# Decoder layer on one core: a deeper pipeline for the attention groups, the maxima turned eight heads at once and split by GpSimd

## The chip, the cores and the metric

One core of one Trainium2 chip runs the whole program. The metric is device time in microseconds (us) of one launch. TensorE (PE) does matrix products and transposes, VectorE (DVE) and ScalarE (ACT) read PSUM and SBUF, GpSimd (POOL) works from SBUF, and the queue of SyncE (SP) issues nearly all DMAs in program order.

## The reference, cut to what matters

Sixteen sequences of 256 tokens, width 256, go through one layer: self-attention with a per-head bias on the key's position, cross-attention over 120 context rows with a mask, and a mixture of eight experts of which each token takes two. A layer norm follows each part.

```
scores = einsum('bqhd,bkhd->bhqk', q, k) / 4 + alibi[h, k]      # 16 heads of depth 16
x = layernorm(x + softmax(scores) v Wo + bo)
x = layernorm(x + cross_attention(x, ctx, mask))                # the same with 120 keys, q from x
x = layernorm(x + top-2 mixture of relu(x w1 + b1) w2 + b2)     # router: x @ gate.T
```

## The kernel before

The first part (`attention`) works sequence by sequence; the second (`experts`) moves all rows by expert and runs 71 blocks of 128 rows. The change is in the first part, but for three semaphores.

**A step.** `iterations` runs `step(i)` for i = -1 to 17 on every engine. Steps 0 to 7 also find the largest expert weight ("max" mode), step 8 makes scales of it (GpSimd's `partition_all_reduce`, then ten small DVE instructions), steps 9 to 16 split one expert's weights in two halves each ("halve" mode, ACT L917 and DVE L771). A step has eight units, u = 0 to 7. In units 0 to 3 the scores of self-attention of sequence i are made, four heads (one group) in a unit, in two halves; in units 4 to 7 those of cross-attention of sequence i-1, one group in a unit.

**The life of a group.** All the scores are made twice. The first time (`scores`, L515 and L532) queries are on the partitions, and DVE takes each row's negated maximum over the keys into `mneg` (`top`, L659 and L664). DVE splits it into three bf16 parts that sum to it (`split_maxima`, L705, L708, L712, L713, eight values a partition). One unit later PE turns the parts (`maxima`, L545), DVE copies them from PSUM (L677) and spreads them into rows 96 to 110 of the group's stacked queries (L684). So the second product (`keyed`, L563 and L571), with keys on the partitions, has the maximum already taken off, and ACT takes the exponential (`exps`, L892 and L896). Two units after its scores the group is weighed with V (`weigh`, L589 and L592; ACT stores the result, L906), three units after them it is turned (`turn_weighed`, L603) and divided by its sum (L681, L693). Scores, second products and weighed sums have one PSUM buffer each: the next group's wait for the reader of the one before.

**The items.** Thirteen projections and transposes stand in the gaps of the units (`GAPS`), each on one of two PSUM banks, in a fixed order for each bank (`ITEMS`); an item waits until the item before it on its bank is read. Q, K, V, Kc, Vc are projections; AOT, O (AOTc, Oc) the attention's output and its projection; T1 turns the first layer norm's output x1 for Qc; T2 and R are the router's. An item's place is (u, half): after the first half of the scores, or after `weigh`. ACT reads Q, K, Qc, Kc (L844), T1, T2, AOT, AOTc (L849) and makes the first bf16 part (L879); GpSimd makes the other two (`split`, L953, L954, L956); SP writes the parts to DRAM and reads them back as stacks (L308, L319). DVE reads V, Vc, O, Oc, R. GpSimd's `deviations` (L964 to L968) turn the moments of O and Oc into the norm's factors, with which ACT makes x1 or x2 (`late`, L866).

Every engine runs its own list in order. In unit u ACT has: the read of the first gap's item, `late`, `exps` of half 0, the first part of that item, the store of the weighed group, `exps` of half 1, the read of the second gap's item, the expert weights.

Of the kernel before, what the change touches and what calls it, by code (L numbers as in the profile page):

```python
# [27 lines left out]
GH = H // NG  # L28
PROD = 96
AUX = 15  # L30
PARTS = 3
NT = T // P
# [8 lines left out]
K_BLOCKS = [0, 0, 0, 1, 1, 2]  # L41
# [67 lines left out]
def attention(nc, ctx, ap, outer, sem):  # L109
# [19 lines left out]
    cT = sb("cT", [P, KT, LC])  # L129
    xrow = sb("xrow", [P, QT, D])  # L130
# [11 lines left out]
    mneg = sb("mneg", [P, QT, GH])  # L142
    mr = sb("mr", [P, QT, GH])
    MTp = sb("MTp", [P, QT, 16], BF16)
    mts = sb("mts", [16, L], BF16)
# [12 lines left out]
    x1bo = sb("x1bo", [P, QT, D])  # L158
# [15 lines left out]
    MT = ps("MT", [16, 1024], BF16)  # L174
# [25 lines left out]
    def wait_apart(eng, name, val, held, count):  # L200
        if not isinstance(val, int) or val > 0:
# [3 lines left out]
    ITEMS = [[("Q", 1), ("T1", -1), ("AOTc", -2), ("Kc", 0), ("T2", -2), ("AOT", 0)],  # L205
             [("Qc", -1), ("Vc", -1), ("K", 1), ("Oc", -2), ("V", 1), ("O", 0), ("R", -2)]]
# [16 lines left out]
    def iterations(step, eng, chain=None, per=0):  # L223
        step(-1, None)
        for i in (0, 1, 2):
            step(i, "max")
        looped(step, eng, 3, 6, "max", chain, per)
        step(6, "max")
# [7 lines left out]
        step(B + 1, None)  # L236
# [11 lines left out]
    def group(u, i, back):  # L248

        n = u - back  # L250
        if n < 0:
            n, i = n + 2 * NG, i - 1
        return (True, i, n) if n < NG else (False, i - 1, n - NG)

    def last(eng, u, i, back, what, per=1):

        for more in range(8):
            if u - back - more < -8:
                return
# [12 lines left out]
    N_Q, N_K = len(Q_RUNS), len(K_BLOCKS)  # L272
    FILL_STEPS = (0, 1, 2, 6, 7)
# [4 lines left out]
    def _(sp):  # L278
# [13 lines left out]
        def later_loads():  # L292
# [4 lines left out]
            sp.dma_start(cT[:, :, :], ap["ctxT"][0].rearrange("(k p) n -> p k n", p=P)).then_inc(sem("ld_cT"), 16)  # L297
# [13 lines left out]
        def read_stack(n, b, blocks):  # L311

            wait(sp, f"wr_{n}", (b + 1) * 16)
            for block0, part0, count in blocks:
                src = dpart[n].rearrange("k a (d m) t -> k (a d) (m t)", m=HM)
                src = src[:, part0 * HD:(part0 + count) * HD, :].rearrange("k p n -> p k n")
                dst = stack[n][block0 * HD:(block0 + count) * HD, :, :].rearrange(
                    "p (k m) t -> p k (m t)", k=KT)
                sp.dma_start(dst, src).then_inc(sem(f"st_{n}"), 16)  # L319

        k_runs = [(n, a, 1) for n, a in enumerate(K_BLOCKS)]
# [35 lines left out]
        def step(i, mode):  # L357
            experts_in(i - 1, mode, 1)
            if on(i):
# [3 lines left out]
            if on(i - 1):  # L363

                wait_apart(sp, "STc", NG * (i - 1), "wr_mask", 16)
                read_stack("ck", i - 1, k_runs)
                sp.dma_start(stack["ck"][PROD:PROD + PARTS, :, :],
                             dmask[bass.ds(i - 1, 1)].rearrange("b a t -> (b a) t").unsqueeze(1)
                             .to_broadcast([PARTS, H, LC])).then_inc(sem("st_ck"), 16)
                write_parts("cq", i - 1)  # L370
                read_stack("cq", i - 1, Q_RUNS)
            if on(i + 1):
                write_parts("q", i + 1)
            if on(i) and not (isinstance(i, int) and i == 0):
                wait(sp, "Vc", i)
                sp.dma_start(cT[:, :, :], ap["ctxT"][bass.ds(i, 1)].rearrange("b (k p) n -> p (b k) n", p=P)
                             ).then_inc(sem("ld_cT"), 16)
            if on(i + 1):
                write_parts("k", i + 1)
                wait_apart(sp, "ST", 2 * NG * (i + 1), "wr_mask", 16)  # L380
                read_stack("q", i + 1, Q_RUNS)
                read_stack("k", i + 1, k_runs)
            if on(i + 2):
                wait(sp, "V", i + 2)
                sp.dma_start(xT[:, :, :], ap["xT"][bass.ds(i + 2, 1)].rearrange("b (k p) n -> p (b k) n", p=P)
                             ).then_inc(sem("ld_xT"), 16)
            if isinstance(i, int) and i < 0:
                later_loads()
            experts_out(i - 1, mode, 0)

# [5 lines left out]
            if on(i):  # L396
                write_parts("ck", i)
            if on(i - 2):
                wait(sp, "x2", i - 1)
                sp.dma_start(YS[0:T, :].rearrange("(b t p) d -> b t p d", t=QT, p=P)[bass.ds(i - 2, 1)]  # L400
                             .rearrange("b t p d -> p (b t) d"), x2s[:, :, :]).then_inc(sem("wr_x2"), 16)
# [1149 lines left out]
```

## Time and profile before

| | us |
|---|---|
| three runs | 1412.86, 1416.01, 1415.66 (median 1415.66) |
| the profiled execution | 1412.27 |
| its span, first to last instruction | 1410.2 |
| attention, start to the last routing item | 0 to 809 |
| steps 3 to 6, each | 43.2 to 43.5 |
| steps 11 and 12, each | 45.2 |
| steps 16 and 17 together | 61.8 |

Step times are distances between the first reduction of maxima (L659) in one step and that in the next: step 1 is 72.90 to 116.50 us, step 4 203.09 to 246.38, step 8 376.62 to 425.73, step 12 565.08 to 610.32, steps 16 and 17 747.30 to 809.10. The experts' part follows at 809 us and uses nothing of the change but three semaphore names.

### The profile page before, as it was taken

What the parts mean: (1) busy time and instruction counts of PE and PEld (TensorE: products, weight loads), DVE (VectorE), ACT (ScalarE), POOL (GpSimd) and SP (SyncE); (2) the same over time, 40 slices, a digit from 0 to 9 for tenths busy, and PEclk for the clock granted to TensorE, in tenths of its full rate; (3) what the DMA queues carried; (4) which work ended last, traced back from release to release, by engine and by line L of the source; (5) the groups of instructions that cost most, each with busy time, mean ns of one, the idle gap of its engine ahead of it and who ended that gap; (6) DMA issues with size and microseconds to landing.
All of it is one profiled execution on the core that took longest, in us unless ns stands there. A gap on an engine that the chain in (4) does not pass through costs nothing. (4 is left out here: it accounts for less than half of the span.)

```text
span 1410.2 us, 32514 instructions
## 1 busy us (share of the span) xinstructions
PE 1091.7 (77%) x9874; PEld 772.1 (55%) x9875; DVE 1022.0 (72%) x2410; ACT 567.4 (40%) x1022; POOL 483.5 (34%) x597
## 2 busy tenths in 40 slices
PE   3778899889888888888885600088999999999980
PEld 2445666666655655565553400066777777777750
DVE  2579999999888989999985340066777777777764
ACT  1344555555545656665563200022323323332324
POOL 1233433433344343534322037612223223223324
PEclk7799999999999999999997555599999999999995
DMA  8489886678756887788754152275222222222227
GB/s 207 108 225 226 230 200 142 157 180 227 174 108 163 235 237 154 207 232 221 202 168 137 68 194 106 100 267 159 42 43 43 41 45 41 41 45 41 43 30 245
DMA packets 160383, 202.20 MB, mean 143 GB/s; under 512 B 30444, under 2 KB 141692, under 8 KB 157067
## 3 DMA queue, kind: packets, MB, share of 16 engines
q1 hardware_dynamic: 145864, 182.92, 48.7%
q0 software_dynamic: 13296, 17.83, 7.5%
q10 hardware_dynamic: 1152, 0.53, 0.2%
q8 instruction: 41, 0.67, 0.2%
q14 instruction: 30, 0.25, 0.1%
HBM read 122.63 MB, written 74.41 MB: 140 GB/s over the span
## 5 line engine op out<-in xcount | busy, mean ns | idle before, releaser
L1177 PE MATMUL HB<-xhi,W 128*128 128x128 f16 x2272 | 292.1, 221 | 21.7 <-issue 16.1
L1177 PEld LDWEIGHTS HB<-xhi,W 128*128 x2272 | 202.2, 98 | 65.8 <-issue 48.2
L1177 PE MATMUL HB<-xlo,W 128*128 128x128 f16 x1136 | 225.0, 220 | 0.0
L1460 POOL DMA_INDIRECT d_sums<-ysc,tok x71 | 111.0, 1563 | 327.3 <-DMA XB<-d_rows 171.7
L892 ACT ACTIVATE PT<-SB 128x1024 f32<-128x1024 f32 x128 | 131.1, 1024 | 138.3 <-PE SB L563 136.3
L659 DVE TENSOR_REDUCE mneg<-SA 128x4 f32<-128x1024 f32 x128 | 156.5, 1223 | 41.6 <-PE SA L515 39.5
L1177 PEld LDWEIGHTS HB<-xlo,W 128*128 x1136 | 111.9, 99 | 50.2 <-issue 0.7
L1370 DVE SCALAR_TENSOR_TENSOR hlo<-HB,hhi 128x512 f16<-128x512 f32 x142 | 98.2, 691 | 55.1 <-ACT hhi L1238 51.1
L1238 ACT ACTIVATE hhi<-HB 128x512 f16<-128x512 f32 x142 | 84.2, 593 | 121.3 <-DVE HB L1362 121.2
L1362 DVE SCALAR_TENSOR_TENSOR HB<-HB,SC,b1c 128x512 f32<-128x512 f32 x142 | 107.1, 754 | 16.7 <-PE HB L1177 11.9
L1246 ACT ACTIVATE ysc<-yb,wv 128x256 f32<-128x256 f32 x71 | 36.1, 508 | 191.8 <-DVE yb L1394 181.6
L563 PE MATMUL SB<-q_stack,k_stack 111*128 111x256 bf16 x512 | 80.2, 280 | 38.0 <-DVE q_stack L684 27.0
L1188 PE MATMUL YP<-W,hhi 128*128 x288 | 109.1, 380 | 0.6 <-DVE yb L1394 0.5
L1188 PE MATMUL R<-W,hhi 128*128 x280 | 106.7, 382 | 1.2
L1159 PE MATMUL XTp<-ident,XB 128*128 128x128 f32 x142 | 29.5, 290 | 96.4 <-DMA XB<-d_rows 96.4
L1355 DVE TENSOR_TENSOR xlo<-XTp,xhi 128x256 f16<-128x256 f32 x71 | 30.0, 423 | 101.0 <-ACT xhi L1230 101.0
L515 PE MATMUL SA<-k_stack,q_stack 99*128 99x256 bf16 x512 | 80.7, 281 | 27.2 <-DMA k_stack<-d_k 16.5
L896 ACT ACTIVATE PT<-SB 120x1024 f32<-120x1024 f32 x64 | 65.1, 1018 | 70.4 <-PE SB L571 70.2
L664 DVE TENSOR_REDUCE mneg<-SA 128x8 f32<-128x960 f32 x64 | 73.6, 1150 | 10.3 <-PE SA L532 10.2
L563 PEld LDWEIGHTS SB<-q_stack,k_stack 111*128 111x128 bf16 x512 | 47.2, 100 | 61.5 <-issue 32.4
L1444 POOL DMA_INDIRECT d_rows<-X2R,posu x64 | 62.0, 969 | 45.9 <-DVE posu L1325 26.8
L515 PEld LDWEIGHTS SA<-k_stack,q_stack 99*128 99x128 bf16 x512 | 49.0, 102 | 47.5 <-DVE mneg L659 18.5
(195 smaller groups left out, 2500.4 us busy)
## 6 DMA issues: line engine op xcount, KB each, us to landing
wst<-in_w SPq DMA_DIRECT2D x32, 1024.0 KB, 10.0
d_w<-w SPq DMA_DIRECT2D x16, 1024.0 KB, 6.7
W<-d_w SPq DMA_DIRECT2D x8, 2048.0 KB, 8.7
k_stack<-d_k SPq DMA_DIRECT2D x96, 128.0 KB, 7.2
XB<-d_rows SPq DMA_DIRECT2D x71, 130.0 KB
d_rows<-fill SPq DMA_DIRECT2D x4, 1950.0 KB, 15.6
d_q<-q_part SPq DMA_DIRECT2D x16, 384.0 KB, 5.8
d_k<-k_part SPq DMA_DIRECT2D x16, 384.0 KB, 2.7
```

The lines of the kernel that those rows point to most:

```text
L515: mm = pe.matmul(SA[:, j, t * L:(t + 1) * L], stack["q"][0:PROD + PARTS, h, t * P:(t + 1) * P], stack["k"][0:PROD + PARTS, h, :], start=Tr ...
L563: mm = pe.matmul(SB[:, j, k * L:(k + 1) * L], stack["k"][:, h, k * P:(k + 1) * P], stack["q"][:, h, :], start=True, stop=True)
L659: dve.tensor_reduce(mneg[:, :, 2 * half:2 * half + 2].rearrange("p t j -> p j t"), SA[:, :, :].rearrange("p j (t n) -> p j t n", n=L), AX. ...
L664: dve.tensor_reduce(mneg[:, :, :].rearrange("p t j -> p j t"), SA[:, :, 0:4 * LC].rearrange("p a (c n) -> p a c n", n=LC), AX.X, ALU.max, ...
L892: act.activation(PT[:, slot, 2 * half:2 * half + 2, :, :].rearrange("p j k n -> p (j k n)"), SB[:, :, :].rearrange("p j n -> p (j n)"), AC ...
L896: act.activation(PT[0:LC, slot, :, 0, :], SB[0:LC, :, :].rearrange("p a (c n) -> p (a c) n", n=L), ACT.Exp).then_inc(sem("Ec"), 1)
L1177: mm = pe.matmul(out, w.rearrange("p e n -> p (e n)"), x[n % 2][:, k, :], start=(k == 0 and half == 0 and x is xhi), stop=(k == KT - 1 and ...
L1188: mm = pe.matmul(YP[n % 2][:, :], hhi[n % 3][:, f, :], w, start=(f == 0), stop=(f == FT - 1))
L1238: act.activation(hhi[n % 3][:, 4 * c:4 * c + 4, :].rearrange("p f n -> p (f n)"), HB[n % 2][:, c, :], ACT.Relu).then_inc(sem("hhi"), 1)
L1362: dve.scalar_tensor_tensor(bank, bank, SC[:, 3:4], b1c[:, bass.ds(e, 1), 4 * c:4 * c + 4].rearrange("p e f -> p (e f)") .unsqueeze(2).to_b ...
L1370: dve.scalar_tensor_tensor(hlo[n % 3][:, 4 * c:4 * c + 4, :].rearrange("p f n -> p (f n)"), HB[n % 2][:, c, :], 0.0, hhi[n % 3][:, 4 * c:4 ...
L1460: pool.indirect_dma_start(YS, bass.IndirectOffsetOnAxis(ap=tok[n % 6][:, 0:1], axis=0), ysc[n % 2][:, :], None, compute_op=ALU.add).then_i ...
```

## The change

1. **Distances.** The second product comes three units after the scores (1 before), the weighed sum four (2), turning and dividing five (3): `KEYED, WEIGHED, TURNED = 3, 4, 5`.
2. **Maxima in pairs of groups.** `mneg` holds two groups (eight heads), doubled. At even units PE turns both groups' 27 rows (3 of ones, 3 x 8 parts), DVE copies them and spreads them over eight heads at once (`spread`): four turns, four copies and four spreads of twice the size in a step, where there were eight of each.
3. **The split on GpSimd.** Four DVE instructions a unit become four GpSimd ones a pair (`split_maxima`), at four fixed places of GpSimd's list.
4. **Cross-attention one sequence later** (i-2, `CROSS = 2`), the items moved and put on other banks, and two more steps at the end (to i = 19).
5. **Stacks in halves of eight heads**, each half waiting only for the groups whose rows it overwrites; the key stack by three reads with a repeated source instead of six. The load of xT moves to the next step's start, a second context buffer `cTv` is added, SP's list is reordered, x1bo has four slots.
6. In the second part, five loads count on semaphores that exist already.

```diff
+GM = H // KT
+AUX = PARTS + PARTS * GM
+KEYED, WEIGHED, TURNED = 3, 4, 5
+CROSS = 2
-    GAPS = {(0, 0): ("Q", 1), (0, 1): ("T1", -1), (1, 0): ("Qc", -1), (2, 0): ("Vc", -1),
-            (2, 1): ("AOTc", -2), (3, 0): ("K", 1), (3, 1): ("Oc", -2), (4, 1): ("Kc", 0),
-            (5, 1): ("V", 1), (6, 0): ("T2", -2), (6, 1): ("AOT", 0), (7, 0): ("O", 0), (7, 1): ("R", -2)}
+    ITEMS = [[("T2", -4), ("O", -1), ("Q", 1), ("T1", -1), ("Vc", -2), ("Oc", -3), ("Kc", -1)],
+             [("AOT", -1), ("R", -4), ("K", 1), ("AOTc", -3), ("Qc", -1), ("V", 1)]]
+    GAPS = {(0, 0): ("T2", -4), (0, 1): ("AOT", -1), (1, 0): ("O", -1), (1, 1): ("R", -4), (2, 0): ("Q", 1),
+            (3, 0): ("K", 1), (3, 1): ("T1", -1), (4, 0): ("Vc", -2), (4, 1): ("AOTc", -3), (5, 0): ("Oc", -3),
+            (6, 0): ("Qc", -1), (7, 0): ("Kc", -1), (7, 1): ("V", 1)}
...
         # PE, one unit
                 if u < NG:
                     scores(u, 0, i)
                     turn_weighed(u, i)
-                    maxima(u, i)
                 else:
-                    maxima(u, i)
                     turn_weighed(u, i)
                     scores(u, 0, i)
                 gap(u, 0, i)
+                maxima(u, i)
                 scores(u, 1, i)
                 keyed(u, 0, i)
                 weigh(u, i)
...
         # DVE, one unit
-                    spread_and_divide(u, i)
+                    divide(u, i)
                     top(u, 0, i)
                 top(u, 1, i)
-                split_maxima(u, i)
+                spread(u, i)
+                gap(u, 0, i)
+        def spread(u, i):
+            mine, b, g = group(u, i, 2)
+            if u % 2 or not on(b):
+                return
+            c, q, d = ("", "q", g // 2) if mine else ("c", "cq", g // 2)
+            wait(dve, f"MT{c}", KT * b + d + 1)
+            dve.tensor_copy(mts[0:AUX, :], MT[0:AUX, 0:L]).then_inc(sem(f"mcopy{c}"), 1)
+            wait(dve, f"mcopy{c}", KT * b + d + 1)
+            dve.tensor_copy(stack[q][PROD:PROD + AUX, GM * d:GM * d + GM, :],
+                            mts[0:AUX, :].unsqueeze(1).to_broadcast([AUX, GM, L])).then_inc(sem(f"aux{c}"), 1)
...
         # ACT
-                if u == 0:
+                if u == 3:
                     late("", i - 1)
-                if u == 5:
-                    late("c", i - 2)
+                if u == 7:
+                    late("c", i - 3)
...
         # GpSimd
+        def split_maxima(u, i):
+            mine, b, g = group(u, i, 0)
+            if not on(b):
+                return
+            c = "" if mine else "c"
+            p0, p1, p2 = (MTp[:, :, 3 + GM * a:3 + GM * (a + 1)] for a in range(PARTS))
+            m = mneg[:, u // 2 % 2, :, :]
+            nothing = minus[:, 2:3].unsqueeze(1).to_broadcast([P, QT, GM])
+            mine2, b2, g2 = group(u, i, 2)
+            if on(b2):
+                wait_apart(pool, "MT" if mine2 else "MTc", KT * b2 + g2 // 2 + 1, "ones", 3)
+            wait_apart(pool, f"max{c}", (2 if mine else 1) * (NG * b + g + 1), "ones", 3)
+            chain(pool.tensor_tensor(p0, m, nothing, ALU.add))
+            chain(pool.tensor_tensor(mr[:, :, :], m, p0, ALU.subtract))
+            chain(pool.tensor_tensor(p1, mr[:, :, :], nothing, ALU.add))
+            pool.tensor_tensor(p2, mr[:, :, :], p1, ALU.subtract).then_inc(sem(f"mparts{c}"), 1)
...
+            split_maxima(1, i)
+            deviations("", i - 1)
             split("q", i + 1)
-            split("cq", i - 1)
+            # x1bo of i - 1
+            split_maxima(3, i)
             if not (isinstance(i, int) and i < 0):
                 split("k", i + 1)
-            deviations("c", i - 2)
-            split("ck", i)
             # xbo of i
-            deviations("", i)
+            split_maxima(5, i)
+            deviations("c", i - 3)
+            split("cq", i - 1)
+            split("ck", i - 1)
+            split_maxima(7, i)
...
         # SP, the two halves of the stacks for the next sequence
             if on(i + 1):
                 wait_apart(sp, "ST", 2 * NG * i + NG, "wr_mask", 16)
                 read_stack("q", i + 1, 0)
                 read_stack("k", i + 1, 0)
             # expert weights in
             if on(i + 1):
                 wait_apart(sp, "ST", 2 * NG * (i + 1), "wr_mask", 16)
                 read_stack("q", i + 1, 1)
                 read_stack("k", i + 1, 1)
```

## Rows read from the trace of the kernel before

**Rows 1.** Windows: stretch; PE, PEld, DVE, ACT, POOL busy; clock; DMA.

```profile
72.90:116.50 43.60, 35.23 (x277) 23.40 (x278) 34.46 (x84) 20.09 (x33) 15.98 (x19) 0.96 0.88 219
...
203.09:246.38 43.29, 38.80 (x325) 26.84 (x325) 39.51 (x99) 23.38 (x40) 17.15 (x23) 1.00 0.70 164
...
376.62:425.73 49.11, 41.45 (x322) 27.53 (x320) 39.15 (x100) 23.39 (x40) 16.76 (x22) 0.93 0.57 131
...
565.08:610.32 45.24, 39.42 (x326) 26.77 (x325) 41.78 (x98) 28.25 (x48) 18.56 (x22) 1.00 0.81 221
...
747.30:809.10 61.80, 36.67 (x184) 23.61 (x184) 23.72 (x63) 19.75 (x33) 7.60 (x13) 0.58 0.36 110
```

**Rows 2.** Waits of DVE in step 12: waited for, us in total, times, longest.

```profile
DVE mneg L659 <- PE SA L515: 0.8, 2, 0.5
```

**Rows 3.** Waits of PE in step 12, the two longest.

```profile
PE SB L563 <- DVE q_stack L684: 2.4, 2, 1.6
PE SB L571 <- DVE cq_stack L684: 1.3, 3, 0.6
```

**Rows 4.** Instruction groups of the whole attention part (0 to 830 us).

```profile
L684 DVE COPY q_stack<-mts 15x1024 bf16<-15x1024 bf16 x64 | 46.0, 719 | 2.0
...
L708 DVE TENSOR_TENSOR mr<-mneg,MTp 128x8 f32<-128x8 f32 x128 | 38.2, 298 | 4.4
...
L545 PE MATMUL MT<-identb,MTp 128*15 128x128 bf16 x256 | 36.6, 226 | 13.4 <-DVE MTp L713 12.2
...
L713 DVE TENSOR_TENSOR MTp<-mr,MTp 128x8 bf16<-128x8 f32 x128 | 30.5, 238 | 4.4
...
L684 DVE COPY cq_stack<-mts 15x1024 bf16<-15x1024 bf16 x64 | 26.9, 421 | 2.0
...
L705 DVE CAST MTp<-mneg 128x8 bf16<-128x8 f32 x128 | 25.8, 202 | 4.4
...
L712 DVE CAST MTp<-mr 128x8 bf16<-128x8 f32 x128 | 24.4, 191 | 3.3
```

**Rows 5.** Timeline of ACT in step 12: start us, us, instruction, idle before.

```profile
566.39 0.84 ACT L844 ACTIVATE q_full<-BK,cols 128x256 f32<-128x256 f32 x2 [2.56 <-PE BK L425]
567.12 1.08 ACT L866 ACTIVATE x1s<-r,shift,rstd 128x256 f32<-128x256 f32 x2
568.10 1.02 ACT L896 ACTIVATE PT<-SB 120x1024 f32<-120x1024 f32 x1
...
569.79 0.61 ACT L849 ACTIVATE x1T<-BK 128x512 f32<-128x512 f32 x1
...
595.01 0.61 ACT L844 ACTIVATE ck_full<-BK,cols 128x120 f32<-128x120 f32 x2
595.65 0.40 ACT L879 ACTIVATE ck_part<-ck_full 128x240 bf16<-128x240 f32 x1
```

**Rows 6.** Timeline of POOL in step 12.

```profile
565.13 0.20 POOL L967 TENSOR_TENSOR shift<-mv,rstd 128x2 f32<-128x2 f32 x1
565.47 0.20 POOL L968 TENSOR_TENSOR shift<-shift,minus 128x2 f32<-128x2 f32 x1
...
596.13 0.65 POOL L953 TENSOR_TENSOR ck_rest<-ck_full,ck_part 128x240 f32<-128x240 f32 x1 [2.47 <-ACT ck_part L879]
...
597.65 0.64 POOL L956 TENSOR_TENSOR ck_part<-ck_rest,ck_part 128x240 bf16<-128x240 f32 x1
```

**Rows 7.** Timeline of PE, steps 11 and 12.

```profile
551.96 1.99 PE L433 MATMUL BK<-wv,xT 128*128 128x256 f32 x8
...
569.96 0.44 PE L603 MATMUL AV<-ident,avs 128*128 128x128 f32 x2 [0.55 <-ACT avs L906]
...
574.52 0.61 PE L563 MATMUL SB<-q_stack,k_stack 111*128 111x256 bf16 x4 [0.55 <-ACT PT L892]
```

**Rows 8.** Timeline of PE, step 16.

```profile
751.76 2.71 PE L425 MATMUL BK<-x1T,cq 128*128 128x256 f32 x8 [0.35 <-ACT x1T L849]
...
769.35 0.96 PE L532 MATMUL SA<-ck_stack,cq_stack 99*128 99x120 bf16 x8 [8.49 <-DMA cq_stack<-d_cq]
```

More of the change, by code:

```diff
@@ L224, in iterations @@
         step(-1, None)
-        for i in (0, 1, 2):
+        for i in (0, 1, 2, 3):
             step(i, "max")
-        looped(step, eng, 3, 6, "max", chain, per)
-        step(6, "max")
+        looped(step, eng, 4, 7, "max", chain, per)
         step(7, "max")
@@ L235, in iterations @@
         step(B, "halve")
-        step(B + 1, None)
+        for i in (B + 1, B + 2, B + 3):
+            step(i, None)
     def looped(step, eng, first, end, mode, chain, per):
@@ L372, in step @@
+            if on(i - 2):
+                for k in range(KT):
+                    wait_apart(sp, "STc", NG * (i - 2) - 2 + 2 * k, "wr_mask", 16)
+                    read_stack("ck", i - 2, k)
+                    read_mask(i - 2, k)
+                    read_stack("cq", i - 2, k)
             if on(i + 1):
                 write_parts("q", i + 1)
[L374 to L377, printed above, removed]
+                write_parts("k", i + 1)
@@ L387, in step @@
[L387 to L389 removed]
+                wait_apart(sp, "ST", 2 * NG * i + NG, "wr_mask", 16)
+                read_stack("q", i + 1, 0)
+                read_stack("k", i + 1, 0)
             if mode == "scale":
@@ L537, in maxima @@
         def maxima(u, i):
-            mine, b, g = group(u, i, 1)
-            if not on(b):
+            mine, b, g = group(u, i, 2)
+            if u % 2 or not on(b):
                 return
             c = "" if mine else "c"
-            wait(pe, f"mparts{c}", NG * b + g + 1)
-            last(pe, u, i, 2, "mcopy")
+            wait(pe, f"mparts{c}", KT * b + g // 2 + 1)
+            mine2, b2, g2 = group(u, i, 4)
+            if on(b2):
+                wait(pe, "mcopy" if mine2 else "mcopyc", KT * b2 + g2 // 2 + 1)
             for t in range(QT):
@@ L698, in split_maxima, with divide @@
-        def split_maxima(u, i):
-            mine, b, g = group(u, i, 0)
-            c = "" if mine else "c"
-            p0, p1, p2 = (MTp[:, :, 3 + GH * a:3 + GH * (a + 1)] for a in range(PARTS))
-            if on(b):
-                wait(dve, f"max{c}", (2 if mine else 1) * (NG * b + g + 1))
-                chain.put(dve.tensor_copy(p0, mneg[:, :, :]))
-            if on(b):
-                chain.wait()
-                chain.put(dve.tensor_tensor(mr[:, :, :], mneg[:, :, :], p0, ALU.subtract))
-            gap(u, 0, i)
-            if on(b):
-                chain.wait()
-                chain(dve.tensor_copy(p1, mr[:, :, :]))
-                dve.tensor_tensor(p2, mr[:, :, :], p1, ALU.subtract).then_inc(sem(f"mparts{c}"), 1)
+        def divide(u, i):
+            mine, b, g = group(u, i, TURNED)
+            if not on(b):
+                return
+            c = "" if mine else "c"
+            turned = AV[:, 0:QT * P].rearrange("p (t j c) -> p t j c", t=QT, c=2 * HD)
+            wait(dve, f"AVT{c}", NG * b + g + 1)
+            chain(dve.reciprocal(rc[:, :, :], turned[:, :, :, HD]))
+            if g == 0:
+                if mine:
+                    wait(dve, "AOTc", b - 2)
+                else:
+                    wait(dve, "AOT", b + 3 if not isinstance(b, int) else min(b + 3, B))
+            dve.tensor_tensor(ao[:, :, GH * HD * g:GH * HD * (g + 1)].rearrange("p t (j c) -> p t j c", c=HD),
+                              turned[:, :, :, 0:HD],
+                              rc[:, :, :].unsqueeze(3).to_broadcast([P, QT, GH, HD]), ALU.mult
+                              ).then_inc(sem(f"norm{c}"), 1)
```

224 lines of the change are left out of this document (110 added, 114 removed).

## The prediction

> **What bounds the kernel now.** I read the busy time by stretches first. The attention part takes 809 us of the 1410 and is cut into steps; the table gives one stretch for each kind. In step 12, which stands for the seven steps that also split weights, DVE is busy for 41.78 of 45.24 us and PE for 39.42; in step 4, which stands for those that look for the largest weight, for 39.51 and 38.80 of 43.29 [rows 1]. The granted clock is 1.00 in both, the upper of TensorE's two levels. The list of waits then says who holds whom: DVE's longest item is 0.8 us in a whole step [rows 2], so what is left of its 45 us is the space between its instructions. PE waits much longer, and the two longest items are stacks that DVE has not yet filled, 2.4 and 1.3 us [rows 3]. So DVE sets the step, and PE is only 5.8 us behind (45.24 - 39.42) [rows 1]. The reader is to see both: DVE is the bound, and what its relief can give ends at PE, whose own waits decide.
>
> **The change part by part.** *DVE.* The four splitting instructions leave it: 25.8 + 38.2 + 24.4 + 30.5 = 118.9 us over sixteen sequences, 7.4 a step [rows 4]. The spreads take 46.0 + 26.9 = 72.9, 4.6 a step [rows 4]. The new four are twice as long: at the undisturbed 421 ns each would cost between 0.42 (nothing for the size) and 0.84 us (all of it); an eight-element cast of 191 ns bounds the fixed part, so I take about 0.65, 2.6 a step, 2.0 less than now [rows 4]. Four short copies of the turned rows go too. DVE's busy 41.8 become about 32: it is no bound any more, and each of its waits can grow by several us without harm.
>
> *PE.* It loses half of its turns of maxima: 36.6 / 16 / 2 = 1.1 us busy [rows 4], about 0.9 where they overlap their neighbours. Nothing else of its work changes. In step 12 it has 39.4 busy and 0.4 of small holes, so 38.9 us of work after; in step 4, 38.1 [rows 1]. Everything now hangs on how long it waits in a step. I went through the eight units of a steady step of the new order by hand, each engine's list with durations of the rows, and found these waits of PE:
>
> (a) *The last split of a step.* `split_maxima(7)` stands in GpSimd's list behind `split("ck")`, and that behind ACT. From the end of Kc on PE (unit 7): ACT reads it, 0.61, makes x2, 1.08, takes the exponential, 1.02, and makes the first part, 0.40 [rows 5]; GpSimd's split of ck takes 596.13 to 598.29, 2.2 us, and the four small operations are 0.34 apart at two elements a partition [rows 6], 1.4 in all at sixteen if size adds nothing, 3 if each is as long as a 240-element one (0.64); I take 1.5. Together 6.8, with some 0.2 for the signals. PE has from there the second product 0.6, the weighed sum 1.0, V 1.99 [rows 7], scores 0.5, a turn 0.4 and T2 0.5, less overlaps 4.8. It then stands at the turn of the maxima: 2.1 us. Behind it in PE's list are the second half of the scores and everything else; DVE waits for that and can afford it.
>
> (b) *Unit 3 to 4.* `late` moves to unit 3, behind the read of K and before the exponential; T1 needs x1, and Vc needs T1's bank read. ACT's list from K's end is 566.39 to 570.40 in the present order (read, x1, exponential, first part, store, read of T1) and here one exponential more, 4.0 + 1.0 [rows 5]; PE's work between K and Vc is 3.5. Waits of T1, second product, turn and Vc together 1.7.
>
> (c) *Unit 2 to 3.* Exponential, first part of q and store come before the turn: 0.75, as one of the same kind costs 0.55 now [rows 7]. (d) *Unit 5.* Oc needs AOTc read by ACT, behind an exponential: 1.02 + 0.61 [rows 5] against a turn and half the scores, 0.9. Before, nothing stood between. (e) *DVE in units 1 and 2*, late with the first reduction behind O's sum and moments: 0.65. (f) *Second halves* of the products where the gap has no item: 0.3 together; such a one is 0.55 now [rows 7].
>
> That is 6.4 us of waits where 5.5 are now. The step becomes 38.9 + 6.4 = 45.3 in "halve" mode, 0.1 more than now, and 38.1 + 6.4 = 44.5 in "max" mode, 1.2 more. The waits on DVE go; waits on ACT and GpSimd take their place.
>
> A rule of the Trainium skill speaks on (a). The row shows the same copy at 421 ns on the cross stack and at 719 ns on the self stack, which runs when GpSimd is busy [rows 4]. The page "SBUF — State Buffer", section "Who interferes with whom", has VectorE and GpSimd share a port pair as an exclusive lock, taken also by a VectorE instruction with two SBUF inputs against a GpSimd read; by it each of the sixteen new operations can stand behind a weight instruction or a spread. The sum is without that; with it, (a) is some 0.7 longer and the fourteen steps 10 us.
>
> *Step 8.* The step is 49.11 us now [rows 1]. GpSimd's reduction over partitions and its start-up keep it from the splits; the first split of the pair then comes about 2.5 us too late for PE, of which I count 1.2 net.
>
> *Fill and drain.* Cross-attention lags one more sequence. Step 0 is bound by loads and stays. Step 1 has no cross work: 43.60 [rows 1] become about 33, 11 less. Step 2 has the cross scores only, 6 less. At the end, from 747.3 on, 61.8 us are left now [rows 1]. Qc of the last sequence comes at 4.5 us of it, the scores 17.6 after that start [rows 8], the end 40 us later. After the change Qc is in unit 6 of step 16, about 18 us in; from it to the scores I count 22 (GpSimd's queue has ck and the split of a pair besides, SP's list a write and a context load), and 45 from there to R, through steps 17 to 19, since each pair waits for two groups and Oc is in unit 5. 18 + 22 + 45 = 85, 23 more. The clock is 0.58 there now and stays low [rows 1].
>
> *DMA, SP.* Bytes are the same but for one small context load. Halves start earlier; SP has some ten issues more, with slack of 3 to 5 us where I followed it. Nothing, with DMA late as a rival.
>
> *Sum*: -11 (step 1) - 6 (step 2) + 4.8 (steps 4 to 7) + 1.2 (step 8) + 0.7 (steps 9 to 15) + 23 (end) = +12.7; step 3 is even. Against the profiled execution's own 1412.3 (span 1410.2 and 2.1 around it): 1425. The median of the runs shown is 1415.66, 3.4 above that execution, with runs from 1412.86 to 1416.01; I don't add the 3.4 and predict 1424.
>
> **The rivals.** *PE is let go (faster).* If half of the waits (a) to (f) are absorbed by each other, since PE's standing at one place lets ACT and GpSimd catch up for the next, a step takes about 42.1 us, 3.2 less, in twelve full steps 38 less: 1386. For it: DVE's relief is large and sure, and the longer distances give every group two units more. Against: (a), (b) and (d) are chains that begin at an item that PE itself has just done, so a late PE makes them late too. It decides when a step's waits fall below 5.4 us ((12.7 / 13) less than 6.4).
>
> *GpSimd, or the stacks, become the bound (much slower).* GpSimd is busy 18.6 us of a step [rows 1] and gets 16 more operations; if they are as long as the 240-element ones or locked out, or if a half stack lands after its scores, a step costs 1.5 more, 20 in all: 1444. For it: DMA is busy 0.70 to 0.88 of a step already [rows 1]. Against: both have long idle stretches.
>
> *The drain is hidden.* If the end costs only 10 more, not 23, my sum gives 1411, no change.
>
> **How the numbers follow.** About 0.2%, 2.8 us, is what a measurement of this kernel can tell from no change. The forecast (waits replaced, a dearer end; 1412 to 1438): 0.44, of which 0.03 fall within 0.2%. Drain hidden: 0.10, 0.05 of it within 0.2%, 0.03 faster, 0.02 slower. PE let go (1375 to 1410): 0.31, faster. The bound moves (1438 to 1460): 0.15. So faster 0.34, same 0.08, slower 0.58; forecast 1424. The range leaves out 0.08 at either side: 1383 to 1446. Cases of both signs are in it; the forecast's own range is 1412 to 1438.
>
> **What would show it.** Right: DVE busy 32 to 33 us a step; PE's waits led by the maxima on GpSimd at about 2 us in each step, then ACT; few on DVE; steps of 44 to 45.5; the last routing item 80 to 90 us after step 15. Wrong: steps under 43, or waits on stacks' DMAs. The step most likely to be wrong is the sum of PE's waits, by thirteen steps a us each.

## The result and the profile after

The change makes the kernel slower: 1487.45 us median (1486.12 to 1488.27) against 1415.84 (1412.86 to 1424.59) of the kernel before on the same chip, a ratio of 1.0494 with a 95% interval of 1.0448 to 1.0541. I had forecast 1424, 1383 to 1446: the direction is right, and the size is wrong by 63 us.

The profiled execution took 1487.3 us, its span 1485.5. The experts' part is as long as before (from the last routing item to the end 600.5 us, 601.3 before), so everything happened in the attention part, which ends at 885.0 instead of 808.9. Distances between the first reductions of the steps say where:

| stretch | before | forecast | after | missed by |
|---|---|---|---|---|
| start to step 0 | 29.5 | +0 | +0.8 | 0.8 |
| steps 0 to 3 | 173.6 | -17 | +21.7 | 38.7 |
| steps 4 to 7 | 173.5 | +4.8 | +8.7 | 3.9 |
| step 8 | 49.1 | +1.2 | +1.7 | 0.5 |
| steps 9 to 14 | 276.4 | +0.7 | +9.6 | 8.9 |
| step 15 to the end of attention | 106.8 | +23 | +33.6 | 10.6 |
| sum | 808.9 | +12.7 | +76.1 | 63.4 |

The windows of the kernel after, one for each kind of step, columns as in [rows 1]: step 1, step 4, step 6, step 8, step 12, and from step 15 on.

```profile
79.61:125.81 46.20, 31.19 (x198) 20.16 (x196) 21.12 (x35) 16.55 (x28) 17.67 (x26) 0.83 0.53 149
225.58:271.94 46.36, 39.68 (x320) 27.32 (x318) 30.69 (x58) 23.43 (x40) 20.86 (x39) 0.96 0.71 204
317.04:362.03 44.99, 38.98 (x319) 27.21 (x318) 30.59 (x58) 23.43 (x40) 20.73 (x39) 0.96 0.62 168
407.82:458.62 50.80, 39.92 (x316) 27.15 (x315) 29.98 (x61) 23.27 (x40) 21.11 (x40) 0.93 0.56 155
602.11:649.20 47.09, 39.82 (x318) 26.91 (x317) 33.80 (x57) 28.30 (x48) 23.19 (x39) 0.96 0.73 204
744.56:885.00 140.44, 99.33 (x651) 65.42 (x649) 65.26 (x135) 57.38 (x96) 34.79 (x76) 0.75 0.40 124
```

DVE did what it should: 33.8 us busy in step 12 instead of 41.78, 30.6 in step 6. The waits of PE that had been the longest before, for the stacks that DVE fills, are gone: over the attention part of the kernel before they were

```profile
PE SB L563 <- DVE q_stack L684: 27.0, 31, 1.9
PE SB L571 <- DVE cq_stack L684: 18.7, 38, 2.0
```

and now they are 0.4 us together. It did not make the step shorter. PE is busy as before, and the step is longer, at a granted clock of 0.96 where it was 1.00. The longest waits of PE over the whole attention part are now (us in total, times, longest):

```profile
PE BK L440 <- DMA xT<-in_xT: 37.8, 11, 6.8
PE SA L532 <- DVE mneg L679: 34.8, 41, 6.2
PE MT L565 <- POOL MTp L982: 33.6, 18, 5.2
PE SA L532 <- DMA k_stack<-d_k: 30.1, 11, 15.2
```

and in step 6 alone:

```profile
PE MT L565 <- POOL MTp L982: 2.0, 1, 2.0
PE BK L448 <- ACT aoT L856: 1.0, 1, 1.0
PE AV L623 <- ACT avs L913: 0.8, 3, 0.4
PE BK L448 <- ACT x1T L856: 0.6, 1, 0.6
```

In step 6, which no late transfer disturbs, these are (a), (d), the turns of weighed groups and a part of (b), as the prediction named them. ("Undisturbed" is said here of steps 5 and 6, in which PE waits for no transfer.) The first line of the whole part is the surprise. Before, PE waited for xT once, 4.9 us at the very start of the program; now 11 times, 37.8 us, of which the start has 5.0, steps 0 to 3 have 19.6 and steps 10 to 14 have 12.2. The key stack had 16.5 and has 30.1. DVE's reductions of the maxima (L679), for which PE waited 10.2 us before, have 34.8, mostly in the first three steps; the part on the prediction returns to them. The SP queue at the end of step 2 (start, length of the issue, line, transfer, instructions):

```profile
171.90 5.46 SPq L365 DMA_DIRECT2D d_rows<-fill  x1
177.40 6.53 SPq L374 DMA_DIRECT2D xT<-in_xT  x1
```

and PE behind them:

```profile
190.86 3.61 PE L440 MATMUL BK<-xT,wq 128*128 128x256 f32 x8 [6.85 <-DMA xT<-in_xT]
```

A fill of the expert rows stands ahead of xT now. Its issue takes 5.46 us and that of xT behind it 6.53, and Q waits 6.85. Then Q's eight matmuls take 3.61 us, while the same product in the form of V took 1.99 [rows 7]: a stall of PE is paid twice, since the clock is at the lower of its two levels behind it (granted 0.53 from 190.86 to 194.40).

### The profile page after: what moved, and what is told of

It reads as the page before. It is cut to its first block and busy times, and to the rows that moved or that the text cites. A ratio compares the mean times of both kernels' runs of the same rounds, so it can differ in the third digit from the quotient of the medians.

```text
span 1485.5 us, 32429 instructions
## 1 busy us (share of the span) xinstructions
PE 1101.0 (74%) x9746; PEld 778.9 (52%) x9747; DVE 888.3 (60%) x1770; ACT 566.9 (38%) x1022; POOL 551.8 (37%) x853
## 5 line engine op out<-in xcount | busy, mean ns | idle before, releaser
L679 DVE TENSOR_REDUCE mneg<-SA 128x4 f32<-128x1024 f32 x128 | 156.6, 1223 | 130.8 <-PE SA L532 130.4
L532 PE MATMUL SA<-k_stack,q_stack 99*128 99x256 bf16 x512 | 86.6, 297 | 64.9 <-DVE mneg L679 34.8
L1405 DVE SCALAR_TENSOR_TENSOR hlo<-HB,hhi 128x512 f16<-128x512 f32 x142 | 98.2, 692 | 55.1 <-ACT hhi L1273 51.2
L979 POOL TENSOR_TENSOR MTp<-mneg,minus 128x16 bf16<-128x16 f32 x64 | 17.1, 268 | 222.5 <-DVE mneg L679 165.3
L1194 PE MATMUL XTp<-ident,XB 128*128 128x128 f32 x142 | 29.5, 290 | 94.8 <-DMA XB<-d_rows 94.7
L532 PEld LDWEIGHTS SA<-k_stack,q_stack 99*128 99x128 bf16 x512 | 46.6, 105 | 98.8 <-DVE mneg L679 52.9
L1390 DVE TENSOR_TENSOR xlo<-XTp,xhi 128x256 f16<-128x256 f32 x71 | 30.1, 424 | 100.0 <-issue 82.7
L583 PE MATMUL SB<-q_stack,k_stack 123*128 123x256 bf16 x512 | 78.2, 275 | 12.6 <-ACT PT L899 10.1
```

What stands on the lines that cost most here:

```text
L532: mm = pe.matmul(SA[:, j, t * L:(t + 1) * L], stack["q"][0:PROD + PARTS, h, t * P:(t + 1) * P], stack["k"][0:PROD + PARTS, h, :], start=Tr ...
L583: mm = pe.matmul(SB[:, j, k * L:(k + 1) * L], stack["k"][:, h, k * P:(k + 1) * P], stack["q"][:, h, :], start=True, stop=True)
L679: dve.tensor_reduce(mneg[:, u // 2 % 2, :, at:at + 2].rearrange("p t j -> p j t"), SA[:, :, :].rearrange("p j (t n) -> p j t n", n=L), AX. ...
L1405: dve.scalar_tensor_tensor(hlo[n % 3][:, 4 * c:4 * c + 4, :].rearrange("p f n -> p (f n)"), HB[n % 2][:, c, :], 0.0, hhi[n % 3][:, 4 * c:4 ...
```

## The experiments

All times are medians of four executions, the ratio is to runs of the kernel before on the same chip. The first table gives the totals, the second where each run spent its attention part.

| run | us | ratio, 95% interval |
|---|---|---|
| after | 1487.45 | 1.0494, 1.0448 to 1.0541 |
| 1. xT ahead of the fills | 1467.34 | 1.0363, 1.0329 to 1.0398 |
| 2. last split ahead of ck | 1484.12 | 1.0482, 1.0447 to 1.0517 |
| 3. split back on DVE | 1475.15 | 1.0438, 1.0396 to 1.0480 |
| 4. runs 1 and 2 together | 1456.84 | 1.0298, 1.0263 to 1.0332 |
| 5. run 4, fills moved | 1451.68 | 1.0264, 1.0224 to 1.0305 |
| 6. run 2, V with its own xT | 1460.99 | 1.0313, 1.0260 to 1.0365 |
| 7. run 6, fills moved | 1452.27 | 1.0274, 1.0234 to 1.0313 |
| 8. run 4, small expert loads | 1442.52 | 1.0188, 1.0150 to 1.0226 |
| 9. before, weight halves on GpSimd | 1455.32 | 1.0282, 1.0244 to 1.0320 |
| 10. run 4, `late` in unit 2 | 1452.77 | 1.0259, 1.0224 to 1.0294 |
| 11. runs 1, 3 and 10 together | 1450.10 | 1.0226, 1.0192 to 1.0259 |
| 12. run 11, fills moved | 1443.50 | 1.0181, 1.0145 to 1.0216 |

| us in steps | 0 to 3 | 4 to 7 | 8 | 9 to 14 | 15 to end |
|---|---|---|---|---|---|
| before | 173.6 | 173.5 | 49.1 | 276.4 | 106.8 |
| after | 195.3 | 182.2 | 50.8 | 285.9 | 140.4 |
| run 1 | 190.3 | 179.0 | 51.3 | 276.5 | 137.5 |
| run 2 | 200.6 | 176.2 | 50.6 | 288.6 | 136.7 |
| run 3 | 192.6 | 178.2 | 44.0 | 288.4 | 135.8 |
| run 4 | 184.9 | 176.0 | 51.8 | 272.4 | 136.5 |
| run 5 | 175.1 | 170.8 | 52.1 | 275.4 | 144.4 |
| run 6 | 185.9 | 175.6 | 51.3 | 278.6 | 137.9 |
| run 7 | 176.0 | 170.8 | 50.9 | 276.7 | 142.0 |
| run 8 | 184.4 | 175.8 | 51.5 | 263.7 | 132.3 |
| run 9 | 174.4 | 174.3 | 51.0 | 308.6 | 114.3 |
| run 10 | 187.9 | 173.0 | 51.2 | 273.9 | 132.6 |
| run 11 | 185.5 | 174.8 | 44.2 | 269.7 | 137.3 |
| run 12 | 174.8 | 170.6 | 43.8 | 273.9 | 143.0 |

**Run 1, xT ahead of the fills.** The load is issued at the end of a step again, ahead of the write of an expert's second half and of the fill. (The kernel before has it a little earlier still, ahead of the expert's other transfers too.)

```diff
                 write_parts("cq", i - 1)
+            if on(i + 2):
+                wait(sp, "V", i + 2)
+                sp.dma_start(xT[:, :, :], ap["xT"][bass.ds(i + 2, 1)] ...).then_inc(sem("ld_xT"), 16)
...
-            if on(i + 1) and not (isinstance(i, int) and i < 0):
-                wait(sp, "V", i + 1)
-                sp.dma_start(xT[:, :, :], ap["xT"][bass.ds(i + 1, 1)] ...).then_inc(sem("ld_xT"), 16)
```

> The changed kernel with one move in SP's list: the load of the next xT stands at the end of a step, ahead of the write of an expert's second half and of the filling of rows (and, at the start, ahead of the later loads), with the same wait on V. Theory A: the place of that load in SP's list is what I had priced at nothing, and costs PE its waits on xT (33 us more than before over the part) and the half clock behind them: 1487 becomes 1440 to 1450, steps 10 to 14 fall from 47 to 49.6 us to about 45, steps 2 and 3 by 6 to 8. Rival B: the DMA engines are full, and xT lands late or something else does in its place wherever it is issued: 1475 to 1487, with waits on stacks or expert weights growing by what xT's lose.

It took 20.1 us off, half of what theory A wanted: 1467.34 lies between the two forecasts. PE's wait for xT fell by 32, from 37.8 us to 5.6 (4.9 in the kernel before), and 20.1 of it came back in time; in place of the rest stand the split on GpSimd, 38.9 (33.6 after), and the cross stack's DMA, 17.5 (5.7 after).

**Run 2, the last split of a step ahead of ck.**

```diff
-            split("ck", i - 1)
             split_maxima(7, i)
+            split("ck", i - 1)
```

> The changed kernel with GpSimd's last two entries swapped: the fourth split of maxima ahead of the split of ck. Theory A: PE's wait for the turn of the maxima in unit 0 (33.6 us in all, 2.0 in a full step) hangs on ck's chain through ACT and GpSimd, as the prediction had it; it goes to under 0.3 a step, and 1487 becomes 1455 to 1465. Rival: other waits of PE fill the place, since ACT is as late as PE: 1475 to 1487.

In a step without disturbance it did all that (a) stands for. Run 2, the step that answers to step 6 above:

```profile
321.95:364.48 42.53, 37.67 (x319) 26.27 (x318) 30.49 (x58) 23.22 (x40) 20.81 (x39) 1.00 0.65 176
```

44.99 became 42.53, 2.5 less: the 2.0 of the wait and the clock behind it. But the whole kernel came out 3.3 us lower, which is the rival's forecast, and the intervals of the two ratios do not tell it from nothing. The waits of PE over the attention part show why:

```profile
PE BK L440 <- DMA xT<-in_xT: 44.7, 12, 7.0
PE SA L532 <- DVE mneg L679: 41.5, 46, 6.1
PE SA L532 <- DMA k_stack<-d_k: 30.0, 14, 16.2
...
PE MT L565 <- POOL MTp L982: 9.4, 4, 4.5
```

The split's 33.6 fell to 9.4, and xT rose from 37.8 to 44.7. Where a transfer is late, PE reaches it earlier and waits longer.

**Run 3, the split back on DVE.** The same pairs, but the four instructions are DVE's again, right behind the first copy of a unit's list.

```diff
         # DVE, one unit
+                split_maxima(u, i)
                 spread(u, i)
...
         # GpSimd
-            split_maxima(1, i)
...
-            split_maxima(3, i)
...
-            split_maxima(5, i)
...
-            split_maxima(7, i)
```

> The changed kernel with the split of the maxima back on DVE, four instructions a pair of groups, all else as changed. It tells what moving it to GpSimd gave. If DVE's time no longer matters (theory A), this is not slower and is faster by the wait of unit 0: 1455 to 1470. If the relief of DVE is worth what it was meant to (rival), it is slower: 1495 to 1520. DVE gets 4 x 4 instructions of about 0.2 us, 3 us a step with what it waits for GpSimd's port.

12.3 us less than the kernel after by the medians, 8 by the ratios, whose intervals overlap; it is between the two forecasts and nearer theory A. In the profiled executions 6.8 us of the difference are step 8. There GpSimd does this in the kernel after:

```profile
416.00 0.38 POOL L998 PARTITION_ALL_REDUCE wg<-wm  x1 [6.10 <-issue]
423.27 0.21 POOL L979 TENSOR_TENSOR MTp<-mneg,minus 128x16 bf16<-128x16 f32 x1 [6.89 <-issue]
```

From 409.89, the end of the fourth small operation, to 423.27 nothing else runs on it. PE waits 6.2 us for the split in that step, 4.3 of it at one place. The other 2 us are the wait (a), which every undisturbed step has. With the split on DVE the step is 44.0 us, 5.1 less than in the kernel before too. In the undisturbed steps the split costs less on DVE (43.4 us) than on GpSimd behind ck (45.0), and more than on GpSimd ahead of ck (42.5).

**Run 4, runs 1 and 2 together.**

> The moves of the first two together. If the two waits are apart they add: 1487 - 40 - 27 = 1420; if each hides the other, 1435 to 1445. Below 1416 only if the steady step falls under 42 us.

30.6 us less than after, where the two alone gave 20.1 and 3.3. The repairs give more than their sum, as they would if xT no longer swallowed what the split gives; but 1456.84 is above both forecasts. The windows of an undisturbed step, and of steps 11 and 12:

```profile
306.55:349.08 42.53, 37.68 (x319) 26.27 (x318) 30.49 (x58) 23.21 (x40) 20.80 (x39) 1.00 0.65 176
534.87:578.40 43.53, 37.30 (x310) 25.64 (x311) 33.98 (x59) 27.57 (x48) 23.23 (x39) 1.00 0.78 216
578.40:626.49 48.09, 40.45 (x324) 27.07 (x322) 33.46 (x58) 28.61 (x49) 22.46 (x39) 0.96 0.72 206
```

Steps 10 to 14 alternate between 43.5 and 46 to 48 us. In the long one PE waits 3.0 us for the cross stack's DMA (0.2 in the short one) and is busy 3.1 us more for the same work. About half of the 3.1 is that the trace has 14 more of its matmuls; for one of them PE is busy 125 ns in the long step and 120 in the short one, at a granted clock of 0.96 and 1.00.

**Run 5, run 4 with the fills moved.**

```diff
-    FILL_STEPS = (0, 1, 2, 3, 7)
+    FILL_STEPS = (0, 7, 8, 16, 17)
```

> The kernel with xT's load moved and the last split ahead of ck (1456.8), and the five writes of padding rows, 2 MB each, moved from steps 0, 1, 2, 3 and 7 to steps 0, 7, 8, 16 and 17. Theory A: steps 1 to 3 (41 to 50 us) are long because these writes stand in SP's list and in the DMA queue ahead of the cross stacks and xT, which the changed order needs within ten us; they fall to 43 to 44, together 12 to 15 us less: 1442 to 1445. Rival: steps 1 to 3 are long because PE's pipeline is still filling, whatever DMA does: within 3 us of 1457.

Windows of its steps 2 and 4:

```profile
119.41:162.76 43.35, 33.75 (x240) 22.72 (x238) 26.61 (x41) 17.35 (x29) 19.94 (x34) 0.88 0.63 162
206.83:249.36 42.53, 37.77 (x320) 26.37 (x318) 30.50 (x58) 23.21 (x40) 20.91 (x39) 1.00 0.63 175
```

Steps 0 to 3 fall by 9.8 us and step 4 by 5.2, to 42.5. So the fills had made steps 2 to 4 47 to 50 us long, as theory A has it. But 11 of these 15 are lost again: 7.9 at the end, where two of the fills now stand in SP's list, and 3.0 in steps 9 to 14. The total is midway between the forecasts.

**Runs 6 and 7, an own copy of xT for V.** V read xT last, so the load of the next xT had to wait for V. With a second buffer it is issued in the middle of the step, behind K; V's own copy comes later.

```diff
+    xTv = sb("xTv", [P, KT, L])
...
-                put_rows(name, xT, wv, QT, P)
+                    wait(pe, "ld_xTv", 16 * b)
+                    put_rows(name, xTv, wv, QT, P)
```

> The changed kernel with the last split ahead of ck, and V reading its own copy of x transposed, so that Q's and K's copy can be loaded from the middle of the step before, behind the first halves of the stacks, instead of at the turn of the steps. One more load of 256 KB a step. Theory A (deadlines, not volume): neither xT nor the cross stacks are waited for in steps 10 to 14, which fall to 43 to 44 us throughout, where the variant with xT's load only moved alternates between 43.5 and 48: 1440 to 1446. Rival B (volume): DMA is full in these steps; with more bytes they stay at 46 to 48: 1455 to 1465.

> Both together: if deadlines are the cause of both, 1425 to 1435, and what is left over the kernel before is the drain (some 30 us), against which stand steps of 42.5 to 43.5 us.

1460.99 is 4.2 above run 4, with intervals that overlap, and 1452.27 is that of run 5. In run 6 PE waits for xT only at the start (5.0 us), but 33.8 us for the cross stack's DMA and 31.6 for the key stack's. So the due time of xT is not the limit: run 6 came out as its rival B, and run 7 missed its 1425 to 1435. That a transfer let go earlier stands in front of another one fits these waits; these two runs do not show it by themselves.

**Run 8, small expert loads.** Run 4 with an eighth of each expert's weights loaded in steps 8 to 15; seven eighths of that load are left out.

> The variant with xT's load moved and the last split ahead of ck (1456.8), where in steps 8 to 15 only an eighth of each expert's weights is loaded (the rest of the tiles keeps old values; all writes to DRAM stay), which takes some 1.8 MB of some 9.6 MB from a step's traffic. Theory A: steps 10 to 14 swing between 43.5 and 48 us because the bulk loads stand in the DMA queue ahead of stacks that the new order needs soon; all fall to 43.5, 10 to 14 us less: 1443 to 1447. Rival (SP's own list is too long): they stay, within 4 us.

14.3 us less than run 4. The window of its step 11:

```profile
529.87:573.36 43.49, 37.81 (x316) 26.19 (x316) 33.82 (x58) 28.05 (x49) 23.15 (x39) 1.00 0.63 179
```

The alternation is gone: steps 9 to 14 are 43.5 to 44.9 each. With less bulk in the queue the same order of instructions runs at its own pace. This is theory A.

**Run 9, the kernel before with the weight halves on GpSimd.** It relieves DVE of another work, which is off the chain of the maxima: in steps 9 to 16 GpSimd scales the weights and subtracts the first half (two instructions for DVE's one at L771). Nothing else changes.

```diff
         # DVE
-                if u:
-                    halves(u - 1, i, mode)
         # GpSimd
+                chain(pool.tensor_tensor(w, w, scale.to_broadcast(list(w.shape)), ALU.mult))
+                ins = pool.tensor_tensor(half_of(k, 1, c), w, hi, ALU.subtract)
```

> The kernel before, with one piece of DVE's work moved to GpSimd that no engine waits for soon: the low halves of the weights in steps 9 to 16 (eight instructions of 0.75 us a step, here two of GpSimd each); splits, distances, items and SP as before. Theory A: DVE's time was a bound in the kernel before and the gain was lost to what came with it; here steps 11 to 14 fall from 45.2 to 41.5 to 43 us, PE next with its 39.4: 1385 to 1400. Rival: DVE's relief is worth nothing because PE's own waits carry the step, or GpSimd blocks DVE's copies by the shared port as much as it relieves it: 1410 to 1425.

Slower, 1455.32, where the forecasts were 1385 to 1400 and 1410 to 1425: steps 9 to 14 take 308.6 us instead of 276.4. DVE has fewer instructions (90 in step 11, 98 in step 12 before) and is busier (43.48 us of 49.06, before 41.78 of 45.24). Some forms of DVE between 560 and 740 us, first the kernel before, then run 9:

```profile
L708 DVE TENSOR_TENSOR mr<-mneg,MTp 128x8 f32<-128x8 f32 x32 | 10.3, 323 | 1.1
...
L712 DVE CAST MTp<-mr 128x8 bf16<-128x8 f32 x32 | 6.2, 195 | 0.8
```

```profile
L712 DVE CAST MTp<-mr 128x8 bf16<-128x8 f32 x28 | 18.5, 660 | 0.7
...
L708 DVE TENSOR_TENSOR mr<-mneg,MTp 128x8 f32<-128x8 f32 x28 | 13.6, 486 | 1.0
...
L684 DVE COPY cq_stack<-mts 15x1024 bf16<-15x1024 bf16 x16 | 11.9, 742 | 0.5
```

A cast of eight values takes 660 ns on the mean instead of 195, the spread of the cross stack 742 instead of 420; that of the self stack is the exception, 658 instead of 829. GpSimd is busy 33.87 of the 49.06 us of step 11. The single instructions show where the means come from. In run 9 the subtraction at L708 takes at most 168 ns in the 10 cases in which no GpSimd instruction overlaps it, and up to 1190 ns in the 18 others; the cast at L712 at most 178 ns in 10 cases, and up to 1070 in 18. PE's waits for the split rise from 12.2 [rows 4] to 48.1 us. GpSimd's own list is longer too, and PE's wait for the cross stack's DMA rises from 11.1 to 15.4. The rule of the Trainium skill that the prediction weighed ("SBUF — State Buffer", "Who interferes with whom": the port pair is an exclusive lock between VectorE and GpSimd) agrees with these rows.

**Run 10, run 4 with `late` at the end of unit 2.** ACT makes x1 one unit earlier.

```diff
-                if u == 3:
-                    late("", i - 1)
...
                 first_part(u, 1, i)
+                if u == 2:
+                    late("", i - 1)
                 weights(u, i, mode)
```

> The variant with xT's load moved and the last split ahead of ck (1456.8), with the making of x1 on ACT moved from unit 3, between K's read and an exponential, to the end of unit 2. Theory: the waits of PE that begin at K in unit 3 (x1 0.5, Vc behind T1's read 0.6, and the second product) go, and quiet steps fall from 42.5 to about 41.4, in all 10 to 14 us: 1443 to 1447. Rival: ACT is only shifted, and the stack reads take what is freed: above 1453.

The undisturbed steps go from 42.5 to 41.7, the total from 1456.84 to 1452.77 on another chip (0.4% by the ratios, whose intervals overlap), between the two forecasts. So (b) was worth about 0.8 of the 1.7 that I gave it.

**Runs 11 and 12, the best of the parts together.** Run 11 has the split on DVE, xT ahead of the fills and `late` in unit 2; run 12 also has the fills of run 5.

> Edit, on the kernel after: the split of the maxima back on VectorE (four instructions a pair, right behind the first copy of each unit's list, as in the earlier run), the load of xT ahead of the fills in its old place, and the first layer norm's items at the end of unit 2. Theory A, the gains add: the split's return gave 12.3 us by itself (1475.15 against 1487.45), and the other two edits stood at 1452.77 with the split on GpSimd, so 1440, of it 7 us in step 8 (51 to 44), since GpSimd's reduction over partitions no longer stands ahead of a split. Theory B, only step 8 and the drain give: with the last split ahead of ck the quiet steps are at 41.7 already, and VectorE's 7 us more of work bring them to 43.4 as in the earlier run, 1.7 us more in each of the three and up to as much in others; then 1449.

> The run before this one plus the fills of the expert rows moved from steps 0 to 3 and 7 to steps 0, 7, 8, 16 and 17. Theory A: as with the split on GpSimd, steps 2 to 4 fall from about 47 to 50 to about 43, 12 us, and the drain and step 9 give 7 of it back: 5 us less than the run before. Theory B: VectorE now carries 39 to 40 us in a step of 43.4, so those steps don't fall below 43.5 and the drain's loss eats the rest: the same within 2 us. Either way it is above the kernel before, since the drain of steps 15 to 19 stays some 25 to 30 us longer than its 106.8.

Run 11 is theory B: by its ratio 0.3% under run 10, with intervals that overlap, with step 8 at 44.2 and the undisturbed steps at 42.6 instead of 41.7. So the split on GpSimd is worth 0.9 us in an undisturbed step, once it stands ahead of ck, and loses 7.0 in step 8. Run 12 is nearer theory A: 6.6 less, steps 3 to 6 at 42.6 each, though step 2 went only from 48.7 to 46.6. It has the lowest ratio of all the versions with the change and is still 1.8% above the kernel before. Its own differences to before are the most telling line of the study: start +1.5, steps 0 to 3 +1.2, 4 to 7 -2.9, step 8 -5.3, 9 to 14 -2.5, and from step 15 on +36.2.

## Why the prediction was wrong, point by point

**The failing step is "DMA, SP: nothing, with DMA late as a rival"**, and beside it "Step 1 ... 11 less. Step 2 ... 6 less". I had followed the slack of the stacks and not the one transfer that the change moves past others: xT goes from the middle of SP's list to the next step's start, behind a fill or an expert's weights. Steps 0 to 3 missed the forecast by 38.7 us, and the wait list gives PE's wait for xT as 2.1, 4.2, 6.5 and 6.8 us in them. Run 1 (xT, 20.1 us off the whole) and run 5 (the fills, 9.8 off steps 0 to 3) show that both are causal. My rival with "a half stack lands after its scores" had the right kind of cause and priced it at 1.5 us a step; PE's wait for xT alone was four times that in steps 2 and 3, and the upper end of that rival, 1460, was still 27 too low.

Run 5, with xT, the last split and the fills all moved, divides the miss. 35.8 of the 63 us are gone. Of the 38.7 in steps 0 to 3, 20.2 are gone and 18.6 stay; steps 4 to 14 are below the forecast by 7; the start is 2.2 and the end 14.6 above it. So two terms besides the one on DMA were mis-sized: the fill and the drain. The term on DMA, put at nothing, measured 20.1 us for xT (run 1) and 5.2 net for the fills (run 5 against run 4); the rest of the 35.8 came with the last split once xT was in time (10.5, run 4 against run 1).

**The fill's gain was a second failing step.** Of the 17 us nothing came, even where xT and the fills are out of the way. In run 5 step 1 takes 41.4 us, 2.2 less than before and not 11, and step 2 takes 43.4, 0.3 more and not 6 less. PE is busy 29.0 us in step 1, less than the 33 that I took for the whole. These are its longest waits there:

```profile
PE SA L532 <- DVE mneg L679: 5.0, 6, 1.3
PE SA L532 <- DMA k_stack<-d_k: 3.7, 1, 3.7
PE SB L583 <- ACT PT L899: 1.9, 5, 0.9
PE MT L565 <- POOL MTp L982: 1.1, 1, 1.1
```

The first is the wait for the reduction that holds the scores' one buffer. It is 12.8 us in step 0 and 5.0 in steps 1 and 2 each, where the kernel before has 3.7 in step 0 and none in the other two. With the second product three units behind the scores and no cross work yet, PE has little to do between two halves of the scores and stands until DVE has read the first: the time that the missing cross work would have filled is waited instead. I had taken PE's work as the length of a step in which PE is not the bound. This is read from the traces; no run has the shorter distances with the rest of the change.

**PE's waits (a) to (f)** were right: 5.7 us in step 6, forecast 6.4. (a): 2.0 forecast as 2.1, and the four operations span 317.95 to 319.26, 1.3 us, forecast 1.5. (d) 1.0 for 0.9. The undisturbed step came out at 45.0 to 45.1 against 44.5 forecast. What I had left out is the clock, 0.96 granted instead of 1.00, which comes back to 1.00 when run 2 removes the wait (a). POOL around (a) in step 6:

```profile
317.36 0.64 POOL L963 TENSOR_TENSOR ck_part<-ck_rest,ck_part 128x240 bf16<-128x240 f32 x1
317.95 0.22 POOL L979 TENSOR_TENSOR MTp<-mneg,minus 128x16 bf16<-128x16 f32 x1
318.32 0.22 POOL L980 TENSOR_TENSOR mr<-mneg,MTp 128x16 f32<-128x16 f32 x1
318.68 0.22 POOL L981 TENSOR_TENSOR MTp<-mr,minus 128x16 bf16<-128x16 f32 x1
319.04 0.22 POOL L982 TENSOR_TENSOR MTp<-mr,MTp 128x16 bf16<-128x16 f32 x1
```

**DVE** was right: 30.6 to 33.8 us busy for "about 32". The spreads of twice the size took 844 and 686 ns, forecast 650: the self stack's is nearer the upper bound.

**The splits and the port.** The sixteen small operations were hardly held up, and the dearer (a) did not come: 268 ns on the mean for the first (7 of 64 took 0.57 to 0.68 us), 220 to 225 for the others, over the whole attention part. What is longer is DVE's own weight instruction, 816 ns before and 1029 now between 560 and 740 us, at more GpSimd work: 0.75 where no GpSimd instruction overlaps it, 1.07 on the mean where one does. DVE is no bound there, and it costs nothing that PE's waits show. In run 9, where it falls on instructions that PE waits for, steps 9 to 14 are 32 us longer.

**Step 8** was right by luck: 50.8, forecast 50.3. The wait behind GpSimd's reduction is 4.3 us and not the 2.5 (1.2 net) of the prediction, and without any wait for GpSimd the step is 6.8 shorter (run 3). That run has the step 5.1 under the kernel before, which I had not forecast and which hides most of it; what in the change gives the 5.1 was not separated.

**Steps 9 to 14**: 0.7 in seven steps became 9.6 in six. With xT and the last split moved (run 4) they are at 272.4, 4.0 under before. With the bulk out of the queue (run 8) they are at 263.7; how far that is under before is not known, since the kernel before was not run without these loads. In undisturbed steps the deeper pipeline does win, 42.5 or 41.7 us for 43.3, once ck and `late` are out of its way. The rival "PE is let go" wanted this of the change as it stands, where a sum of waits below 5.4 us decides; it has 5.7 in step 6.

**The drain**: 33.6 for 23. By my own steps: Qc of the last sequence comes at 817.2, some 27 us into step 16 (about 790) and not 18. Ahead of it in that step PE waits 2.62 us for a split and 2.21 for a cross stack. The clock is no reason: granted 0.75 from step 15 on, where the same stretch before had 0.72. From Qc to the scores at 843.57 it is 26.3 where I said 22, 5.24 of it at the turn of a pair; from there to the end at 885.0 it is 41.4, and I said 45. PE in the drain:

```profile
794.91 0.39 PE L565 MATMUL MT<-identb,MTp 128*27 128x128 bf16 x2 [2.62 <-POOL MTp L982]
...
810.22 0.96 PE L550 MATMUL SA<-ck_stack,cq_stack 99*128 99x120 bf16 x8 [2.21 <-DMA cq_stack<-d_cq]
...
829.77 0.39 PE L565 MATMUL MT<-identb,MTp 128*27 128x128 bf16 x2 [5.24 <-POOL MTp L982]
```

In no run with the change was the end under 132 us, whatever was done to the queue or the split. Where the fills keep their places it is 26 to 34 us longer than before; moving two of them there adds 4 to 8 (runs 5, 7 and 12). What is left when queue and split are repaired points at the lag of one more sequence, the longer distances and the groups in pairs; this is argued and not shown, since no run has `CROSS = 1` or single groups with the rest of the change. Step 0 keeps 2 to 5 us over before in the repaired runs; the wait for reductions in it, 12.8 us for 3.7, is the likely place.

## What to carry to other kernels

A pipeline with one more stage of lag pays its price once, at the end, and its gain once a step. Here the gain was 0.7 to 1.6 us in each undisturbed step of the repaired runs (the change as it stands lost 1.7) and the price 26 to 34 us, with sixteen sequences to spread it over: work that out before anything else. A step in which work is missing is not shorter by that work, if what is left in it is a chain. When an order is rewritten, list for every transfer what now stands ahead of it in its queue; one load moved behind bulk transfers cost 20 us, while the longest wait among the engines that I had followed, the last split, gave 3.3 when it was removed alone and 10.5 behind that repair. And for what relieving the busiest engine can give, my estimate is what the second one waits for it, 3.7 us in the step read here [rows 3], before the new waits are counted; of that an undisturbed step got 1.6 at the best (run 10).

## What the runs showed of the hardware that I had not expected

- An issue can hold its engine for microseconds: SP's issue of xT took 6.53 us behind a fill (5.46 itself), and 6.39 and 6.20 behind two others, where half of SP's issues in the attention part take 0.42 or less and three quarters 0.71 or less.
- A wait of PE costs more than its length, since matmuls behind it run at the lower level of the clock: 2.5 us for the wait of 2.0 that run 2 removes, with the step's granted clock at 0.96 before and 1.00 after it, and 3.61 us for a product of 1.99 behind a wait of 6.85.
- GpSimd's one reduction over partitions shows 0.38 us of busy time and keeps it from any other work for 13.4, 409.89 to 423.27.
- Two long GpSimd instructions in place of one of DVE tripled the mean of a DVE cast of eight values, 195 to 660 ns. Without a GpSimd instruction over it the cast takes at most 178 ns in both kernels; with one, up to 1070 in run 9.
